# Far products of an attention chunk on four column groups of TensorE instead of one 8x512 product

## The reference

```python
q, k, v = proj(Wq, bq), proj(Wk, bk), proj(Wv, bv)        # layernorm(x) @ W.T + b, 16 heads of 16
idx = clip(key - query, -64, 64) + 64
rk, rv = embK[idx], embV[idx]                             # relative positions, 129 rows of 16
logits = einsum('bhqd,bhkd->bhqk', q, k) + einsum('bhqd,qkd->bhqk', q, rk)
w = softmax(logits)
out = einsum('bhqk,bhkd->bhqd', w, v) + einsum('bhqk,qkd->bhqd', w, rv)
x = x + layernorm(out @ Wo.T + bo)
x = x + layernorm(layernorm(x) @ (ternary(Wf) * alpha).T + bf)
```

## Time and profile before

| | |
|---|---|
| median of 3 runs | 2844.34 us |
| the profiled execution | 2847.89 us |
| its span, first to last instruction | 2846.1 us |
| busy TensorE, VectorE, ScalarE, GpSimd | 2648.1, 2036.7, 1573.9, 1018.2 us |
| mean granted TensorE clock | 0.983 of full speed |

### The profile page before, as it was taken

The page is one execution under the profiler, slowest core; times in us unless marked ns, Lnnn a source line. Parts: engine busy times, 40 slices in busy tenths (PEclk is TensorE's granted clock), DMA queues, the critical chain, the costliest instruction groups (busy, mean ns, idle before and its releaser), DMA issues.

```text
span 2846.1 us, 102506 instructions
## 1 busy us (share of the span) xinstructions
PE 2648.1 (93%) x43218; PEld 1971.7 (69%) x43218; DVE 2036.7 (72%) x5187; ACT 1573.9 (55%) x2993; POOL 1018.2 (36%) x2275
## 2 busy tenths in 40 slices
PE   5899999999999999999999999999999999999995
PEld 3567777677776777667776777767777677777773
DVE  4776678676786677866787667776677766787774
ACT  3555556455555555555555565545665455565651
POOL 4113333433334333443234442334323433331025
PEclk8899999999999999999999999999999999999997
DMA  8545644446455464555545556446554456445410
GB/s 224 180 127 169 181 140 129 133 144 181 130 149 145 136 169 131 138 153 160 163 118 144 166 148 162 118 122 175 162 147 126 111 173 180 142 127 145 133 43 27
DMA packets 602999, 409.08 MB, mean 144 GB/s; under 512 B 145578, under 2 KB 602282, under 8 KB 602282
## 3 DMA queue, kind: packets, MB, share of 16 engines
q1 hardware_dynamic: 602538, 402.52, 50.1%
HBM read 206.83 MB, written 194.90 MB: 141 GB/s over the span
## 4 chain that ended last, share of the span: by engine, by line
PE 68%; DVE 16%; issue 5%; ACT 4%; POOL 3%; DMA 0%; SPq 0%; DVEq 0%; ACTq 0%; POOLq 0%
PE logitsT L755 14%; PE oacc L793 14%; PE scores L732 14%; PE logitsT L760 6%; DVE maxes L1012 6%; DVE junk L1009 5%; PE misc L856 4%; PE misc L692 4%; PE misc L818 3%; ACT wxr L1212 2%; PE misc L830 2%; PE misc L706 2%; PE misc L806 2%; POOL rs L1245 1%; DVE stats L915 1%
## 5 line engine op out<-in xcount | busy, mean ns | idle before, releaser
L1009 DVE CUSTOM_DVE_ANT_1 junk<-scores,bands 128x512 bf16<-128x512 f32 x988 | 680.2, 688 | 606.7 <-PE scores L732 588.5
L755 PE MATMUL logitsT<-qs,ks 98*128 98x128 bf16 (+3 forms) x9088 | 995.9, 216 | 33.6 <-ACT wxr L1212 24.6
L1212 ACT ACTIVATE wxr<-logitsT 128x512 f32<-128x512 f32 x1024 | 600.8, 602 | 584.6 <-PE logitsT L755 487.8
L755 PEld LDWEIGHTS logitsT<-qs,ks 98*128 98x128 bf16 (+1 forms) x9088 | 679.6, 99 | 272.4 <-issue 101.3
L1212 ACT ACTIVATE wy<-logitsT 128x512 f32<-128x512 f32 x1024 | 586.3, 596 | 432.1 <-PE logitsT L755 422.4
L732 PE MATMUL scores<-ks,qs 101*128 101x256 bf16 (+10 forms) x4096 | 719.3, 291 | 77.0 <-DVE maxes L1012 39.4
L1012 DVE TENSOR_REDUCE maxes<-scores 128x1 f32<-128x512 f32 x1024 | 701.6, 685 | 2.2 <-PE scores L732 2.2
L732 PEld LDWEIGHTS scores<-ks,qs 96*128 96x128 bf16 (+3 forms) x4096 | 299.7, 100 | 263.0 <-DVE maxes L1012 121.3
L760 PE MATMUL logitsT<-ident,bands 128*128 128x128 f32 x2048 | 468.5, 281 | 0.0
L1240 POOL TENSOR_SCALAR rs<-rs 128x1 int32<-128x1 int32 (+1 forms) x224 | 48.3, 216 | 977.8 <-DVE rs L920 975.3
L760 PEld LDWEIGHTS logitsT<-ident,bands 128*128 128x128 f32 x2048 | 292.7, 143 | 32.9
(11 more groups left out here) (136 smaller groups left out, 2678.8 us busy)
## 6 DMA issues: line engine op xcount, KB each, us to landing
bs<-praw SPq DMA_DIRECT2D x256, 512.0 KB, 4.2
bands<-bs SPq DMA_DIRECT2D x224, 512.0 KB, 4.4
ks<-kd SPq DMA_DIRECT2D x64, 384.0 KB, 4.9
qs<-qd SPq DMA_DIRECT2D x112, 192.0 KB
bands<-bs SPq DMA_DIRECT2D x128, 128.0 KB, 3.4
qd<-qparts SPq DMA_DIRECT2D x64, 192.0 KB, 2.8
kd<-kparts SPq DMA_DIRECT2D x64, 192.0 KB, 2.5
qd<-qparts SPq DMA_DIRECT2D x64, 128.0 KB, 2.6
```

Source lines behind the costliest of these rows:

```text
L755: mm = e.matmul(lt[:, c * P + q0:c * P + q1], kk[0:depth, h, kt * P:(kt + 1) * P], qs[i][0:depth, h, q0:q1], start=q0 == 0, stop=not near, ...
L1009: e.tensor_tensor_reduce(junk[:], scores[:, 0:512].rearrange("p (a c) -> p a c", a=2), banded, 1.0, LOWEST, ALU.add, ALU.max, mx[:, h, 0:1 ...
L1212: e.activation(dst, src, ACT.Exp).then_inc(exp_ready, 1)
```

## The change

The far products of a chunk become four products, each of 128 of the 512 columns of `qf` and each on its own 32 output partitions. `farw` has 32 columns instead of 8 (the eight heads four times over), so that each product fills its 32 output partitions; of these the first 8 rows are used. The result is 128 partitions by 128 columns. The two copies on ScalarE and the three operations on GpSimd have this shape. `write_far` is four DMAs of 8 partitions with 3 parts of 128 tokens, a DMA for each head group and half chunk, and all waits on `far_out` count to 64 for a sequence instead of 32. In `HOLD`, `far` is 1.4 instead of 1.8; this leaves every slot and every bank as they were, and the order of the stages on all five engines is the same as before. What differs in the order is the shape of the instructions, one matmul of 8x512 that is now four of 32x128, and two DMAs that are now four.

```diff
-HOLD = {... "far": 1.8, ...}
+HOLD = {... "far": 1.4, ...}
...
-        headmask, kfar = sb("headmask", [P, HG]), sb("kfar", [P, 2])
-        farw = sb("farw", [P, HG])
+        headmask, kfar = sb("headmask", [P, 32]), sb("kfar", [P, 2])
+        farw = sb("farw", [P, 32])
...
-        fparts0 = oT[0:HG].rearrange("p a i q -> p (a i q)").bitcast(BF16)[:, 0:3 * G * CT].rearrange("p (k g t) -> p k g t", k=3, g=G)
-        fraw = xc[0:HG].rearrange("p i h -> p (i h)").rearrange("p (g t) -> p g t", g=G)
+        fparts0 = oT[:].rearrange("p a i q -> p (a i q)").bitcast(BF16)[:, 0:3 * P].rearrange("p (k t) -> p k t", k=3)
+        fparts = kparts[:].rearrange("p k g t -> p (k g t)")[:, 0:3 * P].rearrange("p (k t) -> p k t", k=3)
+        fraw = xc[:, 0, 0:P]
...
         def far_buf(b):
-            return kparts[0:HG] if b else fparts0
+            return fparts if b else fparts0
...
-                    for g in range(G):
-                        e.dma_start(bass.AP(qd[b % 2].tensor, (g * ROWS + FAR) * HG * S + c * CT,
-                                            [[S, HG], [HG * S, 3], [1, CT]]),
-                                    far_buf(b)[:, :, g, :]).then_inc(far_out[b % 2][c], 16)
+                    for i in range(4):
+                        e.dma_start(bass.AP(qd[b % 2].tensor, (i // 2 * ROWS + FAR) * HG * S + c * CT + i % 2 * P,
+                                            [[S, HG], [HG * S, 3], [1, P]]),
+                                    far_buf(b)[32 * i:32 * i + HG]).then_inc(far_out[b % 2][c], 16)
...
-                        sp.wait_ge(far_out[b % 2][c], 32 * (b // 2 + 1))
+                        sp.wait_ge(far_out[b % 2][c], 64 * (b // 2 + 1))
...
-                    e.matmul(m[0:HG, 0:G * CT], farw[:], qf[:].rearrange("p g t -> p (g t)"), start=True, stop=True).then_inc(far_summed, 1)
+                    for i in range(4):
+                        mm = e.matmul(m[32 * i:32 * i + 32, 0:P], farw[:], qf[:, i // 2, i % 2 * P:i % 2 * P + P], start=True,
+                                      stop=True)
+                    mm.then_inc(far_summed, 1)
...
-                    mv_ = m[0:HG, 0:G * CT].rearrange("p (g t) -> p g t", g=G)
+                    mv_ = m[:, 0:P]
...
-        "headmask": (p[:, None] % HG == np.arange(HG)).astype(f32),
+        "headmask": (p[:, None] % HG == np.arange(32)).astype(f32),
```

More of the change, by code:

```diff
@@ L257 @@
             "tail_wo": "lin_ready", "tail_ff": "lin_ready", "ternary": "threshold_ready"}
-HOLD = {"turn_x": 0.8, "project_q": 2.0, "project_k": 2.0, "far": 1.8, "project_v": 1.8, "band_raw": 0.8, "max_rows": 0.9,
+HOLD = {"turn_x": 0.8, "project_q": 2.0, "project_k": 2.0, "far": 1.4, "project_v": 1.8, "band_raw": 0.8, "max_rows": 0.9,
         "relative": 1.0, "relative_sum": 1.4, "out_norm": 1.5, "tail_attT": 0.6, "tail_x1T": 0.6, "tail_wo": 1.3,
@@ L895, in wait_parts_written @@
             if stage == "project_k" and b:
-                eng.wait_ge(far_out[b % 2][c], 32 * (b // 2 + 1))
+                eng.wait_ge(far_out[b % 2][c], 64 * (b // 2 + 1))
             if b or c:
@@ L1177, in scalar_program @@
                     elif c:
-                        act.wait_ge(far_out[0][c - 1], 32)
+                        act.wait_ge(far_out[0][c - 1], 64)
                     e.activation(far_buf(b)[:, 0], mv_, ACT.Copy)
@@ L1215, in scalar_program @@
                     act.wait_ge(pvY, value["pvY", 2 * pair + 1, 1])
-                    act.wait_ge(far_out[0][NCHUNK - 1], 32)
+                    act.wait_ge(far_out[0][NCHUNK - 1], 64)
                     if pair >= 2:
```

## The result

The changed kernel takes 2825.39 us, the median of four runs (2821.02 to 2828.03), against 2844.49 us for the kernel before in the same session (2843.93 to 2849.77). The ratio is 0.9928 with a 95% interval of 0.9913 to 0.9942, so 19.1 us or 0.7% faster (by the interval, 16.5 to 24.7 us). The forecast was 2827.3 us.

A forecast was written before the change was run, and what follows sets the result against it. TensorE, with 93% busy and 68% of the chain, was taken as the bound. TensorE's 17.1 plus GpSimd's 0.3 made 17.4 us, 0.4 let go: 2844.3 - 17 = 2827.3 us, 8-in-10 range 2821.5 to 2837 us.

The forecast's parts named there:

- The chain as the price list: TensorE's far products: all 28 in the stream on the chain, neighbours idle 1.76 and 1.28 us, so 0.6 us earlier counts.
- the rival in which VectorE takes half of it back: Row maxima on VectorE do not move up in about half the cases; gain 8.5 us, 2836 us; chance 0.13.
- the one in which the groups do not overlap: On TensorE, four quarter matmuls take as long as one, 0.95 us; time stays at 2844 us; chance 0.06.
- the term of 17.1 us: TensorE: each far falls from 1.03 to 0.42 us, 0.61 us less, times 28; ends 14.0 and 19.9 us.
- ScalarE: the term that was mis-sized: ScalarE's two far copies: 0.56 us less a chunk, worth between nothing and 15.7 us, taken as 0.
- Neither copy stands on the chain anywhere: Claim that ScalarE's two far copies are nowhere on the chain of waits; their term was taken as 0.
- behind the far of 203.73 ScalarE has room: The next exponential on ScalarE has sat idle for 1.76 us there, waiting for TensorE.
- GpSimd: Its three far operations fall from 3063 ns to 1.39 us; at most 0.35 us gained through load_x, taken as 0.3.
- the rival with more gain: VectorE's stalls beside GpSimd go and exponentials start sooner: 6.5 us on top, 2821 us; chance 0.10.
- SyncE in the stream: Two further DMA issues a chunk, 0.67 us together, taken as 0; 18.9 us loss if the queue's room were gone.
- Ahead of the stream: Chunks 0 to 3 before the stream: effects sum to -0.1 us, taken as 0, ends -1.5 and +1.5.
- chunk 0 would be 0.9 us earlier: Ahead of the stream: its far write starts at about 29.8 us and its four issues end at 31.1 instead of 31.97.

The follow-up runs named there:

- e1: The changed kernel with each of the four far products issued four times over, 32 records instead of 8; 2843.3 us, ratio 0.9991 to the kernel before.
- e4: The kernel before with the far as four matmuls of 128 columns, all on one column group; 2845.8 us, ratio 1.0001 to the kernel before.
- e8: The changed kernel with each far product issued twice, 16 records instead of 8; 2831.7 us, one run.
- e6: The changed kernel with one more copy of 512 columns on ScalarE ahead of the two far copies; 2830.0 us, one run.
- e7: The changed kernel with a subtract and a cast of 512 columns more on GpSimd; 2825.6 us, one run.
- e3: The kernel before with four smaller DMAs for the far products instead of two; 2847.4 us, ratio 1.0008 to the kernel before.

## Why the prediction was right

- **The chain as the price list.** The step from "on the chain in all 28 cases, with idle neighbours" to "worth its full length" held: e1 gave back 17.9 us for 18.2 us of TensorE. So the rival in which VectorE takes half of it back, 2836 us, did not come, and e4 with the changed kernel settles the one in which the groups do not overlap.
- **The size of the far.** 0.42 us in the timeline, 0.35 on the chain, was forecast, and 0.36 measured; the term of 17.1 us came out as 16.7. The fixed part, read from two sizes of L806 as 0.20 us with the matmul's end (0.13 on the chain), is 0.13 to 0.15 us by e1 and e8. So it was right to weigh the rule of the Trainium skill's "TensorE: Matmul & The Clock Gate", section "Measured speedup vs the span model", by rows; its 0.25 us on the chain would have been 0.11 too short a far, and 3 us too much gain. What the fixed part consists of, a drain of the engine or something else, no run tells.
- **ScalarE: the term that was mis-sized.** Forecast 0, measured about 4 us (3.5 by e6, 4.5 by the difference of the two kernels). Two steps failed. "Neither copy stands on the chain anywhere" is not what the chain shows: behind the fourth far of every sequence it runs over L1179 and L1181, 0.43 and 0.48 us. For the same reason is not the one place where a far's chain leaves TensorE. And "behind the far of 203.73 ScalarE has room" is right of that far, the first of a sequence, and was taken for all. Behind the second and the fourth, ScalarE's queue runs without a gap from one exponential over both copies to the next one, and TensorE waits at its end. One far had been read where there are four places in a sequence.
- **GpSimd.** Forecast 0.3 us with 1.39 us for its three operations; they take 1.17 us, and e7 shows no worth. The stalls of VectorE beside it, the rival with more gain, hardly moved: this instruction of VectorE, now L1038, still has a longest case of 1549 ns with a median of 731.
- **SyncE in the stream.** No loss forecast, none found (e3). An issue of `write_far` takes 300 ns by the median instead of 337. What the Trainium skill says in "DMA: Bandwidth & Descriptors", section "Specifications", of pieces under 512 bytes, that the DMA reads, modifies and writes, costs nothing that the stream of e3 shows.
- **Ahead of the stream.** Forecast 0 with ends of 1.5 us. The scores came 0.95 us later in the changed kernel and 1.4 to 1.9 us later by e3. The step that failed is that chunk 0 would be 0.9 us earlier: its issues started at 29.49 us as worked out, but took 2.32 us instead of 1.3, and its keys were loaded 0.6 us later and not earlier.
- **The sum.** By the stretches it is 16.7 + 4 = about 21 us in the stream, less 1 to 2 us at the start, against 19.1 measured (with an interval of 16.5 to 24.7) and 17 forecast. The mechanism of the main term was right and its size too. That the total came so close is in part luck: two errors of opposite sign, of about 4 and 1 to 2 us, stand behind it. The two profiled executions differ by more, 2846.1 - 2823.5 = 22.6 us in span.

## What to carry to other kernels

A product with few output columns that stands on the chain is worth spreading over column groups, and its price can be worked out beforehand from blocks of two sizes on the same engine: a part per record and a part per block. An instruction of another engine that the change makes shorter can stand on the chain at one of several places where the work recurs and not at the others, or just beside it in a queue; search the whole chain for its line, and look at that queue at every such place, not at one. To find effects of a few tenths of a microsecond, compare stretches between the same instructions of two traces rather than times of the whole kernel, and keep them short enough to hold no place where the clock may fall: the long stretch here varies by 3 us in one trace, the short one behind the fourth far by 0.3.

## What was not expected of the hardware

The same stretch of the same program takes 223.35 to 226.23 us within one execution. It has one place in which TensorE idles, while GpSimd works out the factors of a layer norm and VectorE the rest of a tail. In the kernel before, TensorE is busy for 2.2 of 4 us there in each of the five sequences looked at. In the next 4 us the granted clock is 1.00 in one sequence and 0.59, 0.60, 0.57 and 0.57 in the others (windows: busy us of PE, PEld, DVE, ACT, POOL with their instructions, granted clock, DMA share, GB/s):

```profile
1212.00:1216.00 4.00, 2.21 (x27) 1.18 (x20) 2.99 (x8) 2.17 (x4) 3.60 (x8) 1.00 0.10 34
1216.00:1220.00 4.00, 4.00 (x66) 3.44 (x64) 3.00 (x8) 1.54 (x3) 1.33 (x1) 1.00 1.02 254
```

```profile
1899.00:1903.00 4.00, 2.22 (x34) 1.16 (x23) 2.99 (x8) 2.17 (x4) 3.60 (x8) 1.00 0.14 46
1903.00:1907.00 4.00, 4.00 (x48) 2.82 (x49) 1.69 (x4) 0.86 (x2) 1.49 (x1) 0.57 0.99 260
```

A mean of 0.57 lies near the lower of the two levels, 1.2 GHz. TensorE has records of 66 matmuls in one case and 48 in the other, after the same idle time. The stretch without the fall took 223.35 us, two with it 224.69 and 224.98, so it costs some 1.5 us. The two longest, 226.16 and 226.23 us, lose some 1.3 us more elsewhere; in the one of 226.16 the clock is lower there too:

```profile
1830.00:1834.00 4.00, 3.48 (x49) 2.20 (x47) 3.07 (x9) 1.68 (x3) 3.18 (x10) 0.73 0.03 9
1834.00:1838.00 4.00, 3.82 (x36) 3.02 (x33) 2.81 (x8) 2.85 (x6) 0.11 (x1) 0.84 0.45 111
```

A few such falls more or less would make a good part of the scatter of 3 to 7 us between runs of one kernel; how much of it they make was not counted, and why the clock falls in one sequence and not in another is open.
